# Writing a looped main phase out in full, and putting eight tiles in flight in the expert phase, in a delta-rule attention and top-1 expert kernel

## What is computed

```python
x = x + layernorm(attn(layernorm(x)))
x = x + layernorm(ffn(layernorm(x)))

# attn: q, k, v, gate = x @ Wq.T, ...; beta = sigmoid(x @ Wb.T); alpha = exp(-exp(A_log) * softplus(x @ Wa.T + dt_bias))
def step(S, inp):                                  # for each of 2048 tokens, in order
    k_t, q_t, v_t, beta_t, a_t = inp
    S = S * a_t
    delta = (v_t - einsum('bhd,bhde->bhe', k_t, S)) * beta_t
    S = S + k_t[..., :, None] * delta[..., None, :]
    return S, einsum('bhd,bhde->bhe', q_t, S)
# ctx = rmsnorm(ys, norm_w) * silu(gate); return ctx @ Wo.T + bo

# ffn: logits = l2norm(x) @ l2norm(col_emb).T + sigmoid(gelu(x @ gate_w1 + gate_b1) @ gate_w2 + gate_b2)
weights = one_hot(argmax(logits)) * softmax(logits)          # one expert of 16 for a token
cols = gelu(einsum('bsd,cdn->bscn', x, W_cols) + b_cols) * weights[..., None]
y = cols.reshape(B, S, -1) @ proj_w + proj_b + x
out = layernorm(y) * ln_g + ln_b
```

## Time and profile before

| what | value |
|---|---|
| median of three runs | 4104.34 us (4095.95 to 4114.63) |
| the profiled execution's own time | 4104.04 us |
| its span, from first to last instruction | 4102.2 us |
| mean granted clock of PE | 0.874 of full speed |
| busy: PE, PE's weight loads | 3108.5 us (76%), 2363.5 us (58%) |
| busy: DVE, POOL, ACT | 2832.5 us (69%), 1976.1 us (48%), 1242.5 us (30%) |
| loop of the main phase | about 182 to 3351 us |
| last two steps and the table of tiles | 3351 to 3522 us |
| expert phase | 3522 to 4102.2 us |
| DMA | 438.71 MB, mean 107 GB/s |

### The profile page before, as it was taken

The page is one execution under the profiler, slowest core; times in us unless marked ns, Lnnn a source line. Parts: engine busy times, 40 slices in busy tenths (PEclk is TensorE's granted clock), DMA queues, the critical chain, the costliest instruction groups (busy, mean ns, idle before and its releaser), DMA issues. The chain is left out here.

```text
span 4102.2 us, 151331 instructions
## 1 busy us (share of the span) xinstructions
PE 3108.5 (76%) x59364; PEld 2363.5 (58%) x59364; DVE 2832.5 (69%) x12347; ACT 1242.5 (30%) x2119; POOL 1976.1 (48%) x3051
## 2 busy tenths in 40 slices
PE   5787878788888878888888888888887874455553
PEld 4665656666666666666666666666666653333331
DVE  1676767777777776777777777777776774565664
ACT  2233333333333333333333333333333322111110
POOL 1544444444444444444444444444444441377776
PEclk9899989999999999999999899989998986667776
DMA  3444444444444444444444444444444441566663
GB/s 118 103 108 103 105 105 105 105 100 105 103 104 101 104 97 96 101 99 100 101 100 105 105 105 105 105 105 105 102 108 95 103 98 45 157 156 145 147 148 76
DMA packets 171223, 438.71 MB, mean 107 GB/s; under 512 B 34624, under 2 KB 92608, under 8 KB 153680
## 3 DMA queue, kind: packets, MB, share of 16 engines
q1 hardware_dynamic: 153936, 395.67, 40.8%
q0 software_dynamic: 16640, 33.71, 3.9%
HBM read 357.55 MB, written 75.93 MB: 106 GB/s over the span
## 5 line engine op out<-in xcount | busy, mean ns | idle before, releaser
L408 PE MATMUL work<-xT,w_sb 128*128 128x256 f32 x5120 | 1299.2, 405 | 66.4 <-PEq L399 51.6
L986 POOL TENSOR_TENSOR pairs<-pairs,beta 128x240 f32<-128x240 f32 (+14 forms) x1920 | 865.0, 488 | 791.7 <-POOLq L982 791.7
L408 PEld LDWEIGHTS work<-xT,w_sb 128*128 128x128 f32 x5120 | 990.5, 200 | 268.4 <-issue 127.0
L1210 DVE TENSOR_TENSOR uk<-uk,Ut 128x120 f32<-128x120 f32 (+14 forms) x3840 | 709.9, 227 | 0.0
L1207 DVE TENSOR_TENSOR Ut<-pairs,uk 128x120 f32<-128x120 f32 (+14 forms) x3840 | 690.2, 216 | 6.0 <-DVEq L1198 1.3
L516 PE MATMUL work<-wo_sb,ctxT 128*128 128x512 f32 x512 | 265.8, 668 | 68.3 <-PEq L399 68.3
L1055 POOL DMA_INDIRECT xs_rows<-xfw,slot x64 | 63.9, 999 | 369.5 <-POOLq L1053 359.7
L1194 DVE TENSOR_TENSOR uk<-vT,uk 128x128 f32<-128x128 f32 x256 | 63.3, 293 | 240.4 <-DVEq L1316 180.7
L768 ACT ACTIVATE qraw<-work 128x512 f32<-128x512 f32 x128 | 76.0, 594 | 489.9 <-ACTq L767 489.9
L970 POOL TENSOR_TENSOR Sd<-S,eg_end 128x512 f32<-128x512 f32 x64 | 67.5, 1055 | 322.0 <-POOLq L969 318.6
L516 PEld LDWEIGHTS work<-wo_sb,ctxT 128*128 128x128 f32 x512 | 107.3, 215 | 195.5 <-issue 193.8
(11 more groups left out here) (193 smaller groups left out, 5780.0 us busy)
## 6 DMA issues: line engine op xcount, KB each, us to landing
pairs<-pair_rows SPq DMA_DIRECT2D x512, 480.0 KB, 7.8
w_sb<-xs_rows SPq DMA_DIRECT2D x80, 258.0 KB, 2.8
w_sb<-in_w_cols SPq DMA_DIRECT2D x80, 256.0 KB, 4.0
w_sb<-in_proj_w SPq DMA_DIRECT2D x80, 256.0 KB, 4.2
xt<-in_x SPq DMA_DIRECT2D x66, 256.0 KB, 3.8
pair_rows<-Ak SPq DMA_DIRECT2D x64, 256.0 KB, 2.1
x<-in_x SPq DMA_DIRECT2D x64, 256.0 KB, 11.2
out<-x SPq DMA_DIRECT2D x64, 256.0 KB, 9.9
```

The source lines that it names most:

```text
L408: mm = pe.matmul(w[:, half * BT:(half + 1) * BT], w_sb[:, f, j * D + hg * P:j * D + (hg + 1) * P], xT[:, f, :], start=(f == 0), stop=(f == ...
L986: ins = nc.gpsimd.tensor_tensor(a, a, beta[:, :, t:t + WID[t0]], ALU.mult)
L1210: link(v.tensor_tensor(uk[:, g, at + 1:at + 1 + n], uk[:, g, at + 1:at + 1 + n], Ut[:, g, 0:n], ALU.subtract), behind=1)
```

## The change

The 15 turns of the main loop are written out on all five engines, so that no engine jumps back there. In the written-out steps many calls of `step` stand in another order, on PE, DVE, ACT, POOL and SP. `TURNS` is changed to match. `proj_b` is added to the rows on POOL before the scatter, and taken off again by ACT when it copies the transposed rows. The expert phase has 8 tiles to a loop turn, 10 turns, and works in pairs with stages skewed by one and two pairs; the last `z` is made by ACT.

```diff
-MQ = 4
+MQ = 8
+NPR = MQ // 2
+LAG = 2
...
@@ sync: step
+                if after:
+                    store(block)
                 if ahead:
                     write_rows(0)
                     fetch_pairs(0, 0)
-                if after:
-                    store(block)
...
-            with sp.Fori(0, NT - 3) as i:
+            for i in range(NT - 3):
...
@@ tensor: step
-                if ahead:
-                    project("qk", 1, 0, 0)
-                    project("qk", 1, 0, 1)
                 if after:
                     output_projection(1)
                 if chain:
                     state_to_outputs(0, 1)
                 if ahead:
+                    project("qk", 1, 0, 0)
+                    project("qk", 1, 0, 1)
                     squares_sum(1)
+                if chain:
+                    change_state(0, 0)
+                if ahead:
                     pe.wait_ge(s["lax_ready"], 1)
                     pe.sem_inc(s["lax_ready"], -1)
                     decays(0)
                     decays(1)
                 if chain:
-                    change_state(0, 0)
                     change_state(0, 1)
...
@@ tensor: expert phase
+            def tiles_of_loop(last):
+                for u in range(MQ):
+                    neurons(u)
+                    if not (last and u == MQ - 1):
+                        turn_rows((u + 1) % MQ)
+                    columns_result(u)
...
@@ scalar: expert phase
-                    link(nc.scalar.activation(xsT[u % 2].rearrange("p k t -> p (k t)"), m_tp[u % 2], ACT.Copy))
+                for f in range(KD):
+                    ins = nc.scalar.activation(xsT[u % 2][:, f, :], m_tp[u % 2][:, f * P:(f + 1) * P], ACT.Identity,
+                                               bias=minus_pbT[:, f:f + 1])
+                link(ins)
...
+            def last_norm(k):
+                act.wait_ge(s["m_zr"], 1)
+                act.sem_inc(s["m_zr"], -1)
+                for u in (2 * k, 2 * k + 1):
+                    link(nc.scalar.activation(z[u], ya[u], ACT.Identity, scale=zr[:, u:u + 1], bias=znm[:, u:u + 1]))
+                    act.sem_inc(s["m_ya_free"], 1)
+                    act.sem_inc(m_z_ready[k], 1)
...
@@ gpsimd: step
+                    link(nc.gpsimd.tensor_tensor(xfw[:, :, 0:D], xfw[:, :, 0:D], pb_sb[:].unsqueeze(1).to_broadcast([P, TB, D]), ALU.add))
                     for tb in range(TB):
                         nc.gpsimd.indirect_dma_start(
...
@@ gpsimd: expert phase
+            def tiles_of_loop(first, added):
+                for k in range(NPR):
+                    first_std(k, added)
+                    if not (first and k < 1):
+                        second_std((k - 1) % NPR)
+                    if not (first and k < LAG):
+                        add_rows((k - LAG) % NPR)
                 link.restart()
...
@@ vector: step
+                    decay_products(1)
                 if ahead:
                     alpha_argument()
-                if chain:
-                    decay_products(1)
...
-                if chain:
-                    add_to_state()
                 if ahead:
                     scale(1)
...
@@ vector: expert phase
+            def tiles_of_loop(first):
+                for k in range(NPR):
+                    add_to_rows(k)
+                    if not (first and k < 1):
+                        norm_rows((k - 1) % NPR)
                 link.restart()
```

More of the change, by code:

```diff
@@ L564, in step @@
                 if chain:
+                    state_to_u(0, 0)
                     state_to_u(0, 1)
+                if after:
+                    chunk_to_outputs(NC - 1, 1)
+                if chain:
+                    key_products(1, 0)
                 if ahead:
@@ L663, in step @@
                     gate_hidden()
-                if chain:
-                    change_state(1, 0)
                 if ahead:
@@ L670, in step @@
                     gate_logits(0)
-                if chain:
-                    change_state(1, 1)
-                if after:
                     gate_logits(1)
@@ L690, in _ @@
             step(0, True, False, True)
-            with pe.Fori(0, NT // 2 - 1):
+            for _ in range(NT // 2 - 1):
                 step(1, True, True, True)
@@ new lines, in turn_rows, with neurons @@
+            def turn_rows(u):
+                pe.wait_ge(m_xs[u], 16)
+                pe.sem_inc(m_xs[u], -16)
+                pe.wait_ge(s["m_t_free"], 1)
+                pe.sem_inc(s["m_t_free"], -1)
+                for f in range(KD):
+                    mm = pe.transpose(m_tp[u % 2][:, f * P:(f + 1) * P], xs[u][:, f * P:(f + 1) * P], ident)
+                mm.then_inc(s["m_t"], 1)
+            def neurons(u):
+                pe.wait_ge(m_wc[u], 48)
+                pe.sem_inc(m_wc[u], -48)
+                pe.wait_ge(s["m_xsT"], 1)
+                pe.sem_inc(s["m_xsT"], -1)
+                pe.wait_ge(s["m_h_free"], 1)
+                pe.sem_inc(s["m_h_free"], -1)
+                for f in range(KD):
+                    mm = pe.matmul(m_hp[u % 2], wc[u][:, f, :], xsT[u % 2][:, f, :],
+                                   start=(f == 0), stop=(f == KD - 1))
+                mm.then_inc(s["m_h"], 1)
@@ L734, in _ @@
+            turn_rows(0)
+            with pe.Fori(0, NM // MQ - 1):
+                tiles_of_loop(False)
+            tiles_of_loop(True)
         @block.scalar
@@ L883, in step @@
                     act.sem_inc(s["ss_ready"], 1)
+                if ahead:
+                    act.wait_ge(s["sg_free"], 1)
+                    act.sem_inc(s["sg_free"], -1)
+                    link(sigmoid("gate", 1, sg[:]))
+                    act.sem_inc(s["gate_ready"], 1)
+                if after:
                     copy_turned("xfT", xfT, s["xfT_ready"], 0)
@@ L932, in _ @@
             step(0, True, False, True)
-            with act.Fori(0, NT // 2 - 1):
+            for _ in range(NT // 2 - 1):
                 step(1, True, True, True)
@@ new lines, in tiles_of_loop @@
+            def tiles_of_loop(first, last):
+                for k in range(NPR):
+                    for u in (2 * k, 2 * k + 1):
+                        activate(u)
+                        if not (last and u == MQ - 1):
+                            copy_turned_rows((u + 1) % MQ)
+                    if not (first and k < LAG):
+                        last_norm((k - LAG) % NPR)
+                link.restart()
+            copy_turned_rows(0)
+            tiles_of_loop(True, False)
+            with act.Fori(0, NM // MQ - 2):
+                tiles_of_loop(False, False)
@@ L962, in _ @@
+            tiles_of_loop(False, True)
+            for k in range(NPR - LAG, NPR):
+                last_norm(k)
         @block.gpsimd
@@ L1078, in _ @@
             step(0, True, False, True, None)
-            with pool.Fori(0, NT // 2 - 1) as i:
+            for i in range(NT // 2 - 1):
                 step(1, True, True, True, i * (2 * ROW) + ROW)
@@ L1142, in _ @@
+            add_rows(NPR - 2)
+            second_std(NPR - 1)
+            add_rows(NPR - 1)
+            for k in range(NPR):
+                pool.wait_ge(m_add[k], NM // MQ * 32)
         @block.vector
@@ L1396, in step @@
                     solve_half(1, 1)
+                    add_to_state()
+                if ahead:
+                    next_tokens_norm()
                 if after:
@@ L1401, in step @@
                     rsqrt(rstd[:], ve[:], nt1[:])
-                if ahead:
-                    next_tokens_norm()
-                if after:
                     logits_of_columns()
-                if chain:
-                    add_to_state()
-                if after:
                     choose_columns()
@@ L1437, in _ @@
             step(0, True, False, True)
-            with dve.Fori(0, NT // 2 - 1):
+            for _ in range(NT // 2 - 1):
                 step(1, True, True, True)
```

316 lines of the change are left out of this document (130 added, 186 removed).

## The result

The changed kernel takes 4084.39 us (median of 20 runs, 4049.78 to 4111.57), the kernel before 4108.98 us (20 runs): ratio 0.9945, 95% interval 0.9924 to 0.9966. The forecast was 3854 us. The sign is right, the size is not: 230 us are missing, and they are missing in one place.

What follows compares the result with a forecast made beforehand. Main loop and expert phase were taken as chains of waits through several engines, none full. From 4102.2 us, -75 (main loop) and -175 (expert phase) gave 3852, plus 1.8 around the span: 3854 us; range 3780 to 3955.

Steps and rivals of the forecast that it cites:

- The expert phase: Expert tiles: eight in flight and pairs open the ring of waits, 6.76 to 4.7 us a tile, -175 us with the drain.
- The main phase: Main loop: a step of 103 us against 105.5, over 31 steps rounded to -75 us.
- The jump: Main loop's jump back: removing it at 14 places saves 1.4 us each, 20 us in all.
- (a): Main-loop step: earlier output_projection and half of change_state, later add_to_state end the wait for su; -3.0 us where it occurs.
- (b): Main-loop step: key_products and x1 statistics ahead of the gate product end the wait for kkq; net -2.2 us.
- (c): Main-loop step: decay_products(1) fills the wait for the alpha logits; -1.0 us.
- (f): SP in the main loop: store ahead of write_rows(0), its rows ready some 18 us earlier; cost 0.
- (d): Tail of the main-loop step: all of change_state waits for delT ahead of gate_hidden, PE idle some 5 us; net +1.8 us.
- (e): POOL in the main loop: adding proj_b, 2.9 us ahead of the scatter, is covered by a wait; cost 0 to 0.7 us.
- Two more for fetch gaps: Main-loop step: gaps of 2 to 3 us hit a chain without slack, so 2 us are taken back, 101 to 103.
- the main loop gives nothing: Rival, chance 0.15: the main loop's jump stall and (a) to (c) are absorbed, or (d) takes them; 3919 us.
- Slower: Rival, chance 0.02: PE idle ahead of change_state lowers its clock, 14 us more a main-loop step, 4290 us.

Runs made afterwards that it cites:

- e3: Changed kernel with the old order of calls and PSUM turns, main loop still written out on all five engines: 0.9411 of the kernel before, 3859 us.
- e11: e3 with only the middle of the step (qk projections, first state update, late add_to_state) in the new order: 0.9453 of the kernel before.
- e14: e3 with one PE edit, key products of the first chunk ahead of the state products for the outputs: 0.919 of the kernel before, 3780.15 us.
- e9: e3 with one SP edit, the step's output stored ahead of writing the next rows and fetching the next pairs: 0.9572 of the kernel before.
- e10: e3 with only the start of the step (last chunk's outputs and decay_products(1) first) in the new order: 0.9524 of the kernel before.
- e16: e3 with both PE state updates ahead of the gate network's products and DVE's late add_to_state right behind its solve: 0.9623 of the kernel before.
- e17: e14 plus an unneeded 2.1 MB DRAM copy in each step, right behind the token loads: 0.9355 of the kernel before.
- e1: Changed kernel with the main loop of all five engines put back as a loop, new order kept: 1.0188 of the kernel before, 4176 us.
- e7: e3 with only the end of the step (from key_products(0) on) in the new order: 0.9531 of the kernel before, 3922 us.
- e18: e14 with the first chunk's key products earlier still, first ahead of the last gate projection, second right behind it: 0.9234 of the kernel before.

## Why the prediction was right and wrong

**The expert phase** was right: from the end of the tile table to the end 183 us were saved (581.1 to 398.1) for 175 forecast, at 4.47 us a tile against 4.7. It runs near the DMA limit, as the sum had it, with the engines 94% busy in the steady part. That makes 4.2 us a tile with full engines, so the floor of 4.35 was a little high. POOL is busy 3.3 us a tile, as forecast, but not busiest: DVE has 3.6. The drain did not shrink by 10 us: it is 33 us for 32.6.

**The main phase** was the failure: -75 forecast, +156 measured at the 30th start. The runs split it: order +198 (3309.4 to 3507.3), writing out -64 (3373.6 to 3309.4), and +22 that the looped old order has over the kernel before (3351.4 to 3373.6), where only GpSimd's bias addition and the buffers differ. By the ratios the order costs some 220 us and writing out gives some 80. In the forecast's own terms, a step was to be 4.4 us shorter by waits taken away and 2 us longer by fetch gaps, at an unchanged clock. Measured against the kernel before, by PE's time, the step is 4.7 us longer: PE's waits are the same in sum, late instructions cost 2.9 and slower matmuls 1.9. So the gains did not come, and the clock had been put at nothing. Step by step of the forecast:

- *The jump, -20.* Mechanism right, size wrong by a factor of three to four. I took the 1.4 us between the two kinds of step as the cost of a stall; but steps on both sides of a jump share it, and one kernel's kinds of step can't be compared as if the other had no stall. "Written-out code is fetched as the loop's was" held. The Trainium skill (Runtime: NRT & Kernel Launch, Instruction fetch mechanics) says that fetch runs ahead in sequence, and calls the cost of crossing the boundary of a 16 KiB block "mostly hidden". The trace does not agree: e3, all straight code in the main phase, still has 198 us of gaps in 27 steps.
- *(a), -3.0 a step.* A step that failed. The wait for su at the first place did go (2.5 us a step before, 0.4 in the changed kernel), but it moved: in e11 the third solve waits 2.4 us a step more and the transposes 1.5 more. The forecast took this delay to be "no more than what is gained" and still booked -3.0. The middle alone gives a step of 103.8 for 104.0, and a ratio no better.
- *(b), -2.2.* Its first half is right and larger: the key products alone gave -3.5 us a step (e14; -2.9 by the ratio). In the changed kernel it does not show, as the wait for kkq there is 162.5 us; with the new end alone it was 52.8. Which of the other moves brings it back no run isolates.
- *(c), -1.0, and (f), 0.* The steps that failed outright. I priced both by who waits for them and not by what they start. Both start a fetch earlier, onto matmuls whose instructions are then late. (f) alone costs 0.016 (e9). The part with (c) in it costs 0.011 (e10), and DVE's wait for the alpha logits, which (c) was to fill, is 76.7 us there for 82.3 in e3. That (c) is what costs in e10 is argued from the trace above; no run has it alone.
- *(d), +1.8.* Right in kind ("PE is idle there for some 5 us": 4.7), too small: 3.4 us a step (e16; 2.8 by the ratio). The 3 us by which the logits were to come later are right (2.9).
- *(e), 0 to 0.7.* The addition takes 2.3 us on POOL, for 2.9. No run isolates its cost; the looped old order has a step 0.7 us longer than the kernel before.
- *Two more for fetch gaps.* Right to take, and too little: 2.9 us a step against the kernel before, 3.3 against e3. The order changes where the gaps fall. PE's time in the 27 steps says what the order cost. The stretch of e3:

```profile
400.19:3209.11 2808.92, 2369.91 (x49179) 1835.61 (x49167) 2081.53 (x9855) 976.67 (x1647) 1387.76 (x2106) 0.92 0.45 104
```

The changed kernel's is 168 us longer: 88 us more of late instructions, 48 us more of PE's waits (71 more for delT, less of others) and 33 us more busy for the same matmuls.

Of the rivals, "the main loop gives nothing" was nearest, and it was not low enough. "Slower" had the right place, PE's wait ahead of `change_state`, and a clock that falls behind it (0.50 to 0.59 above), but a single mechanism was not what came: the clock's share of the loss is 51 us, and the rest is spread over several moves.

## What to carry to other kernels

When a call is moved, write down which transfers it starts, and which dense stretches of another engine's instructions then run while the DMA engines are full; an earlier start is no gain by itself. Change a hand-made order one part at a time: of these moves one was worth 0.022 and the others, if they add up, took some 0.075. The whole then looked like almost no change. A stall behind a loop's jump has to be priced against a kernel without the jump, not against the steps between.

## What I had not expected of the hardware

- A piece of TensorE's instructions can be 8 us late in straight code, with no branch near. Each of the 1779 pauses of 1 us and more ends 2.1 to 3.5 us behind the start of a 16 KB piece on queue q8.
- Such pauses go with the kernel's own transfers: with PE's code unchanged, one move on SP takes the pauses at the last state update from 1 in 27 steps (e3) to 15 (e9), and a copy that nothing uses takes those between 50 and 70 us from 23 to 49 us (e17).
- Where PE pauses more, its granted clock is mostly lower, and its matmuls take longer. In the 27 steps the clock is 0.933 in e14 (165 us of late instructions), 0.918 in e3 (198), 0.881 in the changed kernel (286) and 0.864 in e1 (358). Late instructions don't set it alone: e7 has 0.897 with 164 us of late instructions but 303 us of other waits, and e18 has 0.904 with 181 and 195, less of both than e3; why, is open.
- Writing out the main phase on five engines did not add to the gaps: 214.5 us in the looped old order, 198.0 written out.
